# PE's low pass of a group one group later: a three-pass adjacency product on one core

## The reference, cut to what matters

```python
# x: 10000 x 128, adj: 10000 x 10000, all fp32
h = item_feat @ W_item.T + b_item                 # 10000 x 128
b = layernorm(x) @ W_user.T + b_user
x = x + relu(adj @ h + b)
# a mixture of 8 experts (128 -> 512 -> 128, relu), one expert a row, with a capacity
x = x + ffn(layernorm(x))
```

## Time and profile before

| | |
|---|---|
| median of 3 runs | 1460.2 us (1459.67 to 1460.77) |
| profiled execution | 1460.03 us, of it a span of 1458.2 us |
| busy share of the span | PE 94%, DVE 80%, ACT 68%, POOL 34% |
| granted TensorE clock, mean | 0.978 of full speed |
| HBM traffic | 421.5 MB read, 23.5 MB written, 305 GB/s over the span |

### The profile page before, as it was taken

The page is one execution under the profiler, slowest core; times in us unless marked ns, Lnnn a source line. Parts: engine busy times, 40 slices in busy tenths (PEclk is TensorE's granted clock), DMA queues, the critical chain, the costliest instruction groups (busy, mean ns, idle before and its releaser), DMA issues. The chain is left out here.

```text
span 1458.2 us, 20861 instructions
## 1 busy us (share of the span) xinstructions
PE 1371.8 (94%) x6318; PEld 1108.3 (76%) x6318; DVE 1172.4 (80%) x1694; ACT 986.5 (68%) x990; POOL 491.6 (34%) x426
## 2 busy tenths in 40 slices
PE   7999999999999999999999999999999994899992
PEld 6888887877878778778787787877877873678771
DVE  7998797887977979779788797797977973387774
ACT  5687676766766768677676676776766751788860
POOL 0010303313133032230322303403233066288887
PEclk9999999999999999999999999999999997899996
DMA  9999898988989989889898898988988973323220
GB/s 336 355 401 375 292 393 310 383 336 316 390 317 355 351 314 389 329 313 384 317 380 338 310 394 310 370 341 316 392 323 324 388 277 96 85 80 92 75 63 3
DMA packets 88371, 434.33 MB, mean 298 GB/s; under 512 B 22526, under 2 KB 24070, under 8 KB 88328
## 3 DMA queue, kind: packets, MB, share of 16 engines
q1 hardware_dynamic: 70376, 421.55, 77.0%
q0 software_dynamic: 17952, 12.25, 3.2%
HBM read 421.51 MB, written 23.50 MB: 305 GB/s over the span
## 5 line engine op out<-in xcount | busy, mean ns | idle before, releaser
L432 ACT CAST a_hi<-raw 128x2000 fp32r<-128x2000 f32 (+1 forms) x400 | 736.5, 1846 | 253.8 <-DMA raw<-adj_m 186.8
L590 DVE TENSOR_TENSOR a_lo<-raw,a_hi 128x2000 fp32r<-128x2000 f32 (+1 forms) x400 | 866.6, 2212 | 22.5 <-ACT a_hi L432 12.1
L922 PE MATMUL bank<-a_hi,h_hi 128*128 128x500 f32 (+1 forms) x1580 | 636.0, 403 | 0.5 <-ACT a_hi L432 0.5
L924 PE MATMUL bank<-a_hi,h_lo 128*128 128x500 f32 (+1 forms) x1580 | 614.3, 389 | 0.0
L934 PE MATMUL bank<-a_lo,h_hi 128*128 128x500 f32 (+1 forms) x1580 | 430.5, 392 | 22.2 <-DVE a_lo L590 22.2
L934 PEld LDWEIGHTS bank<-a_lo,h_hi 128*128 128x128 f32 (+1 forms) x1580 | 293.7, 188 | 100.5 <-DVE a_lo L590 33.8
L922 PEld LDWEIGHTS bank<-a_hi,h_hi 128*128 128x128 f32 (+1 forms) x1580 | 297.5, 188 | 72.4 <-issue 12.8
L924 PEld LDWEIGHTS bank<-a_hi,h_lo 128*128 128x128 f32 (+1 forms) x1580 | 297.9, 189 | 58.4 <-issue 4.4
L800 POOL TENSOR_TENSOR xrs<-xve,neghalf 125x4 f32<-125x4 f32 x20 | 37.9, 1893 | 461.2 <-DVE xve L603 461.2
L320 POOL TENSOR_TENSOR carrier_pool<-ones 125x1 f32<-125x1 f32 x52 | 47.8, 919 | 387.9 <-DVE slot L703 363.6
L887 POOL DMA_INDIRECT out<-raw,toki x128 | 137.4, 1073 | 35.9 <-issue 34.3
(11 more groups left out here) (112 smaller groups left out, 897.0 us busy)
## 6 DMA issues: line engine op xcount, KB each, us to landing
raw<-adj_m SPq DMA_DIRECT2D x380, 1000.0 KB, 7.3
raw<-adj_m SPq DMA_DIRECT2D x20, 500.0 KB, 5.0
raw<-records SPq DMA_DIRECT2D x32, 202.1 KB
early<-items_t SPq DMA_DIRECT2D x19, 256.0 KB, 4.7
xb<-x SPq DMA_DIRECT2D x20, 224.0 KB
early<-w SPq DMA_DIRECT2D x8, 258.5 KB, 3.6
early<-w SPq DMA_DIRECT2D x8, 256.0 KB, 3.0
out<-raw,toki POOLq DMA_INDIRECT x128
```

The lines of the kernel that those rows point to most:

```text
L432: nc.scalar.copy(a_hi[:, g % HI_RING, 0:m], raw[:, g % RAW, 0:m]).then_inc(hi_ready, 1)
L590: v.tensor_tensor(a_lo[:, g % LO_RING, 0:m], raw[:, g % RAW, 0:m], a_hi[:, g % HI_RING, 0:m].bitcast(F32), ALU.subtract).then_inc(lo_ready, 1)
L922: nc.tensor.matmul(acc[q][:, 0:BLOCK], h_hi[0:m, k * HID:(k + 1) * HID], a, start=(k == 0), stop=False)
L924: last = nc.tensor.matmul(acc[q][:, 0:BLOCK], h_lo[0:m, k * HID:(k + 1) * HID], a, start=False, stop=False)
```

## The change

PE takes the low pass of a group two steps behind its high pass in place of one: step g is the high pass of group g and the low pass of group g - 2, and steps 0 and 1 take the low passes of groups 18 and 19 of the block before. At the end both last groups are taken after block 19. `total`, which runs once, gets a wait of its own for `run_ready`, the one that `count` behind it has. Nothing is added or removed on the other engines, and no buffer gets larger.

```diff
+BEHIND = 2
@@ total
+                pe.wait_ge(run_ready, m + 1)
@@ body of PE
                     high_part(b, q, g)
-                    if g > 0:
-                        low_part(b, q, g - 1)
+                    if g >= BEHIND:
+                        low_part(b, q, g - BEHIND)
                     elif not fixed or b > 0:
-                        low_part(b - 1, 1 - q, GROUPS - 1)
+                        low_part(b - 1, 1 - q, GROUPS + g - BEHIND)
@@ after the blocks
-            low_part(BLOCKS - 1, 1, GROUPS - 1)
+            for g in range(GROUPS - BEHIND, GROUPS):
+                low_part(BLOCKS - 1, 1, g)
```

## The result

The changed kernel takes 1485.7 us (median of 4, 1482.5 to 1486.5) against 1459.9 us before: slower by 1.70%, interval 1.57 to 1.82%. Forecast were 12.3 us more, measured are 25.7. The profiled execution is the lowest of the four, 1482.47 us with a span of 1480.6 us, 22.4 us above that of before.

The account below looks back on a forecast made before the run. It took a loop through PE, DVE and POOL, 59.35 us a block, as the bound. 17 x 0.63 + 1.6 = 12.3 us on the profiled 1460.03 us gave 1472.3 us, range 1461 to 1482.

Parts of the forecast that it names:

- The release of the buffer: DVE's `a_lo` ring: low pass 3 ends 3.13 us later, delaying low part 7; PE's wait grows from 1.32 to 1.75 us.
- A block longer by 0.63 us: Blocks 2 to 18: high pass 14 starts at 658.37 instead of 657.74, so the loop is 59.98 us against 59.35.
- The cast of group 14: ACT, behind `x1_offset` and `normalize_x1`: hidden before, now ends at 658.30, after high pass 14 would start at 658.17.
- The 0.07 us for the signal: Between ACT's cast of group 14 ending at 658.30 and PE's high pass 14 starting at 658.37.
- rival (d): Loads for casts of groups 16 to 18 come late, up to 0.5 us a block more: 1480.8 us, chance 0.18.
- The one low pass that it does less in block 0 it does more at the end: PE over the whole run: matmul count unchanged, the low pass saved first is paid last, so no net cost.
- Block 19: Last block, priced by itself: late casts of groups 18 and 19 cost 1.6 us, bounds 0 and 2.5.
- (a): PE's gap at low pass 11 vanishes, blocks 57.9 us, 25 us less in 18 blocks: 1435 us, chance 0.02.
- (b): The `a_lo` release doesn't hold low part 7; DVE's loop sets the block, 0.1 to 0.5 us shorter: 1454.6 us, chance 0.10.
- What would show it: Trace signs: low part 7 at 17.15 us, PE's wait 1.75 us, blocks about 60.0 us, a short new wait for ACT.

Follow-up runs that it names:

- the release alone: Kernel before, PE's order kept, but DVE waits for one low pass more before it writes an `a_lo` buffer: 1554.4 us, ratio 1.0642.
- Filling the wait: Changed kernel with six more matmuls, result unused, on PE between high pass 13 and low pass 11: 1475.4 us, ratio 1.0118 to the kernel before.
- low pass 3 where it was: Changed kernel, but low passes of groups 0 to 3 run one step behind, the others two: 1463.9 us, ratio 1.0022 to the kernel before.
- one line on POOL or on DVE: Kernel before with `x1_scale` ahead of POOL's indirect DMAs: 1436.4 us; or with `x1_offset` behind low part 11 on DVE: 1434.0 us.
- the count moved: Changed kernel with PE's `count` and `total` after step 3 instead of step 4: 1484.6 us, ratio 1.0184 to the kernel before.

## Why the prediction was wrong

The way was right and the size was not: 12.3 us forecast, 25.7 measured, and the median lies above the range.

- **The release of the buffer** (low part 7 at 17.15 us, PE's wait of 1.75 us, 23.24 us between them): right, 17.18, 1.76 and 23.24. The kernel with the release alone shows the cause.
- **A block longer by 0.63 us**: 0.70 measured, 11.9 us in 17 blocks where the forecast had 10.7. The cast of group 14 was late as forecast, and PE's first matmul behind it is followed by the next only after 0.33 us instead of 0.23. The 0.07 us for the signal, which came from no row, were 0.05.
- **What failed first: a term that wasn't in the sum.** I priced PE's wait by its length alone. A wait that grew from 1.32 to 1.76 us was followed, in some blocks, by a granted clock of 0.50. It made 4.7 us in the profiled execution, and the mean granted clock of the other three was 0.970 to 0.973 against its 0.975. Filling the wait brought the median from 1485.7 to 1475.4. The length of the wait alone doesn't tell when this happens: with `assign` ahead of low part 7 in the order of before, PE waited 1.2 to 1.9 us at low pass 11 of each block and the clock never fell there.
- **The late loads, rival (d)**: one block of seventeen, block 7, lost 1.05 us, where (d) had up to 0.5 us in each. As a rival it was wrong; as a term of the sum it is small.
- **"The one low pass that it does less in block 0 it does more at the end"**: wrong. Ahead of block 2 nothing became shorter (142.22 against 141.83): in block 0, PE's idle time grew from 0.47 to 1.32 us, about as much as the low pass that is gone. The low pass more at the end counts in full. That is 1.3 us.
- **Block 19**: 1.6 us forecast beside that low pass. The last high pass ends 64.31 us into the block instead of 59.74, so 4.6 found; the low pass adds 0.9, and the stage behind is 1.2 shorter, for a reason not followed, which makes the 4.3. The cast of group 18 ended there 18.19 us behind `x1_offset` and not 16.98, and a stretch at the lower clock came behind PE's wait of 1.85 us.
- **The rivals (a) and (b)**, the faster ones, fall with the trace of the changed kernel: low part 7 starts 0.11 us behind low pass 3 in each of blocks 2 to 18, and DVE idles 0.48 to 0.92 us ahead of it. The kernel with low pass 3 where it was doesn't price them, since low part 8 is held there instead.
- **What would show it** was met in each point that I named, but for four of the seventeen blocks, which are longer than 60.0 by the falls and the late load. The new wait for ACT is short: the cast makes high pass 14 start 0.18 us late, and 0.01 to 0.11 of it shows as idle time.

## What to carry to other kernels

A consumer that runs one step later gets its input one step later and gives its buffer back one step later. With a ring of fixed size this only shifts the slack from one side to the other, so follow the release round the loop, to the same instruction of the next turn, before you count the gain. Follow the next buffers of the ring too: with the first one freed early again, the one behind it took over. Where several loops are about equally long, look for what they share: here it was DVE's wait for POOL, and one line on POOL or on DVE won what the two orders of PE tried here did not. And price a wait on PE that gets longer with the clock behind it.

## What the runs showed of the hardware

- The granted clock fell to 0.50 behind waits of PE of 1.6 us by the trace in three blocks of seventeen (in five with the count moved) and stayed at 1.00 behind the same wait in the others. It fell in eight of seventeen with waits of 2.5 us and in each with 4.3 us. It never fell in these blocks with waits of 1.0 to 1.5 us in the kernel before, nor with 1.2 to 1.9 us in that kernel with `assign` moved. A fall cost 1.57 us of a block behind the 1.6 us wait and up to 2.7 behind the long one. What decides between blocks with the same wait isn't shown.
- An indirect DMA's issue on POOL takes 1.19 us with DVE idle. Where it meets DVE's subtraction of two SBUF tensors it takes up to 3.33 us and ends some 1.1 us behind the subtraction, which takes 2.23 to 2.32 us either way. In the kernel with `assign` moved in the changed order, a start less than 0.045 us behind the subtraction's was never held, and a later one always was, in 17 blocks. With `x1_scale` first and DVE busy all through, POOL's busy time rose from 491.6 to 671.7 us, and nothing waited for it.
